# Moving the experts' result stores from the ACT queue to the SP queue

## The reference

```python
E, K, H, CAP = 64, 4, 128, 128          # 64 experts, 4 per token, D = 512
xb = zeros((E, CAP, D)).at[eid, pos].set(flat[tok], mode='drop')
h  = silu(einsum('ecd,edh->ech', xb, Wg)) * einsum('ecd,edh->ech', xb, Wu)
yb = einsum('ech,ehd->ecd', h, Wd)
y  = yb[eid, minimum(pos, CAP - 1)] * (w * valid)[:, None]
out = zeros((N, D)).at[tok].add(y)      # and shared experts are added
```

## Time and profile before

| what | value |
|---|---|
| median of 3 runs | 1286.22 us (1281.49 to 1287.89) |
| the profiled execution | 1287.89 us, span 1286.2 us |
| busy: PE, DVE, ACT, POOL | 85%, 58%, 38%, 44% of the span |
| mean granted TensorE clock | 0.945 |
| `experts` loop | about 947 to 1187 us of the span |
| HBM traffic | 141.23 MB read, 77.59 MB written |

### The profile page before, as it was taken

How to read it: one execution, slowest core, us unless ns; L and a number is a source line. 1 busy time by engine, 2 the same in 40 slices (tenths; PEclk the granted TensorE clock), 3 DMA queues, 4 the chain that set the end, 5 groups by cost and what they waited for, 6 DMA issues and landing times. The chain is left out here.

```text
span 1286.2 us, 19956 instructions
## 1 busy us (share of the span) xinstructions
PE 1095.3 (85%) x5479; PEld 757.0 (59%) x5479; DVE 745.0 (58%) x1760; ACT 486.0 (38%) x865; POOL 570.1 (44%) x754
## 2 busy tenths in 40 slices
PE   3998999999858999997798499999178998888984
PEld 2555555555246777773496276675066766666752
DVE  4678788886337888885556377575412222222565
ACT  2455555555217888885321101212022222221000
POOL 6365565565334666676125456454400000000775
PEclk9999999999958999999799699999679999999988
DMA  9544334541444333332421030220379999995776
GB/s 313 194 164 148 111 125 157 179 163 58 149 150 144 107 107 106 106 106 96 155 67 61 29 110 24 66 75 11 111 262 337 326 355 340 349 349 175 219 234 201
DMA packets 112117, 210.26 MB, mean 163 GB/s; under 512 B 15549, under 2 KB 23741, under 8 KB 112058
## 3 DMA queue, kind: packets, MB, share of 16 engines
q1 hardware_dynamic: 86842, 149.65, 34.8%
q0 software_dynamic: 16000, 43.13, 10.6%
q10 hardware_dynamic: 9216, 16.78, 3.4%
HBM read 141.23 MB, written 77.59 MB: 170 GB/s over the span
## 5 line engine op out<-in xcount | busy, mean ns | idle before, releaser
L1975 POOL DMA_INDIRECT y<-ytab,take x64 | 69.3, 1083 | 275.7 <-POOLq L1814 256.5
L953 POOL TENSOR_TENSOR m_down_lo<-wo,m_down_hi 128x512 fp32r<-128x512 f32 x80 | 133.1, 1683 | 80.6 <-ACT m_down_hi L1028 80.6
L2040 PE MATMUL bank<-flat_hi,w_hi 128*128 128x512 f32 (+1 forms) x320 | 115.8, 362 | 12.9 <-DVE sh_h_b L2051 6.3
L471 PE MATMUL bank<-win,vT 128*128 128x512 f32 x256 | 124.7, 600 | 0.0
L1931 DVE TENSOR_TENSOR stage_gate<-stage_gate,bank 128x128 f32<-128x128 f32 x64 | 18.5, 288 | 166.4 <-ACT stage_gate L1902 166.4
L2040 PE MATMUL bank<-flat_lo,w_hi 128*128 128x512 f32 (+1 forms) x320 | 113.3, 354 | 0.0
L2040 PE MATMUL bank<-flat_hi,w_lo 128*128 128x512 f32 (+1 forms) x320 | 113.0, 353 | 0.0
L641 DVE TENSOR_REDUCE negmax<-bank 128x1 bf16<-128x512 f32 x128 | 86.9, 679 | 41.4 <-PE bank L478 41.0
L564 ACT ACTIVATE win<-bank 128x512 f32<-128x512 f32 x128 | 69.4, 594 | 99.1 <-PE bank L463 98.6
L1042 DVE TENSOR_TENSOR m_up_lo<-w,m_up_hi 128x1024 fp32r<-128x1024 f32 x80 | 99.2, 1241 | 10.3 <-ACT m_up_hi L1015 8.4
L1869 PEld LDWEIGHTS bank<-ident,m_x 128*128 128x128 f32 x256 | 36.7, 208 | 97.2 <-DMA m_x<-tab 86.1
(11 more groups left out here) (286 smaller groups left out, 2601.7 us busy)
## 6 DMA issues: line engine op xcount, KB each, us to landing
m_x<-tab SPq DMA_DIRECT2D x104, 256.0 KB, 3.2
tab<-zeros SPq DMA_DIRECT2D x16, 1024.0 KB, 10.3
ytab<-summary ACTq DMA_DIRECT2D x64, 256.0 KB, 4.9
ytab<-m_y SPq DMA_DIRECT2D x40, 256.0 KB, 2.0
wout<-in_ctx SPq DMA_DIRECT2D x64, 128.0 KB, 2.6
w<-in_L_ffn_wi SPq DMA_DIRECT2D x16, 512.0 KB, 5.4
wo<-in_L_ffn_wo SPq DMA_DIRECT2D x8, 512.0 KB, 6.8
wout<-in_ctx SPq DMA_DIRECT2D x16, 256.0 KB, 3.2
```

What stands on the lines that cost most here:

```text
L471: nc.tensor.matmul(pO[s * 2 + h][:], vT[:, s, sb_, h:h + 2, :].rearrange("p a c -> p (a c)"), probs[:, sb_ % 2, h, :], start=(sb_ == 0), s ...
L953: nc.gpsimd.tensor_tensor(dn_lo[:, m, :], row(wo0, e * MB + m), dn_hi[:, m, :], ALU.subtract).then_inc(dn_lo_ready, 1)
L1975: nc.gpsimd.indirect_dma_start(y1[:, t % RING, k, :], None, T["ytab1"], bass.IndirectOffsetOnAxis(take1[:, t, k:k + 1], 0)).then_inc(gathe ...
L2040: last = nc.tensor.matmul(out, w[:, k, s, wc], x[:, d, cols], start=(d == 0 and part == 0), stop=(d == DB - 1 and part == 2))
```

## The change

The wait for `y_ready` and the issue of the store move from the end of ACT's step to the end of SP's step, behind the loads of the step. The final wait for all stores moves too. The semaphore, the ring and the address stay.

```diff
@@ SP
                 if valid(e, n=E1) and (not isinstance(e, int) or e >= W_EARLY):
                     need(sp, y_full, i)
                     load_expert(sp, A, T, (q - 1) % W_RING, e)
+                if valid(i - 1, n=E1):
+                    n = (q - 1) % RING
+                    need(sp, y_ready, i)
+                    sp.dma_start(T["ytab1"][bass.ds((i - 1) * CAP1, CAP1), :], y[:, n, :]).then_inc(stored[n], 16)
 
             steps(sp, step, E1, W_RING, W_RING - 1, 1)
+            for s in range(RING):
+                sp.wait_ge(stored[s], 16 * E1 // RING)
@@ ACT
                     need(act, h_ready, i - 1)
                     nc.scalar.activation(g[:, s, :], pH[s][:, 0:CAP1], ACT.Silu).then_inc(g_ready, 1)
-                if valid(i - 1, n=E1):
-                    n = (q - 1) % RING
-                    need(act, y_ready, i)
-                    act.dma_start(T["ytab1"][bass.ds((i - 1) * CAP1, CAP1), :], y[:, n, :]).then_inc(stored[n], 16)
 
             steps(act, step, E1, RING, 1, 1)
-            for s in range(RING):
-                act.wait_ge(stored[s], 16 * E1 // RING)
```

## The result

The changed kernel took 1297.72 us in the median of 4 runs (1292.33 to 1299.58), the kernel before 1283.87 in 4 (1281.49 to 1287.89). The ratio is 1.0091, with a 95% interval of 1.0062 to 1.0120: slower by 0.9%, where no change was forecast. It compares means, over 23 executions of the changed kernel; the two medians alone would give 1.0108. The time lies inside the stated range (1273 to 1300), on the side that had a chance of 0.20.

What follows compares the result with a forecast made beforehand. It took DMA and TensorE as coupled, with the rows' landing bounding two loop steps. Terms summed 0 + 0 + 0 + 0 + 0 = 0 against the profiled 1287.89 us; it predicted the median, 1286 us, range 1273 to 1300.

Steps and rivals of the forecast that it cites:

- circle of waits: In the loop, two steps last at least issue delay, rows' landing and one unstalled step: 0.1 + 3.9 + 3.50 = 7.5 us.
- exchange rate: In the loop, a rows' landing longer by x costs x/2 in every step; a shorter one gains x/2 down to 3.50 us.
- unstalled step: A loop step in which TensorE doesn't wait, taken as 3.50 us from the trace, 1098.86 to 1102.36.
- bound of a gain: Most the loop could gain if TensorE's step bound it: (3.77 - 3.50) x 63 = 17 us.
- the traffic: Loop's DMA transfers: same bytes in another order, 0 for the rows' landing, Wd landing sooner; cost 0.
- The store's lateness: Store in the loop issued 1.1 us later, its buffer rewritten only four steps, 15 us, later; cost 0.
- The first rival: Store on q1 ahead of each rows' load counts in full: +20 us, 1306; chance 0.20 together with the clock rival.
- The clock: Second rival: long TensorE stalls lower its clock, 1.5 us each, ten more add 15 us; chance 0.20 with the first rival.
- The faster rival: Rows get the DMA engines for themselves, 0.17 us a step: -10 us, 1276, at most -17; chance 0.24.
- ACT's relief: ACT's queue loses a wait and an issue, 0.34 us per step, covered by TensorE's own work; gain 0.
- SP's issue: Store's issue takes some 0.5 us of SP's queue per step, covered by its 1.72 us slack; cost 0.
- the end of the loop: Last two stores go out on SP behind their copies, before GpSimd starts: 0, give or take 0.3 us.

Runs made afterwards that it cites:

- The square: Store's queue by issue time, against the kernel before (q10, behind Wg): q10 behind Wd 1.0137, q1 behind Wg 1.0062, q1 behind Wd (the changed kernel) 1.0128.
- the pad: Changed kernel with an unused DRAM tensor of 1317 rows between tab1 and ytab1: 1.0112 of the kernel before, the changed kernel beside it 1.0096.

## Why the prediction was wrong

**The bound.** The circle of waits was the right frame, and it was the change's whole loss: with the rows' lead one or two steps longer the changed kernel is 2.1 and 2.5% faster than the one before. Its exchange rate held in size from end to end, not from kernel to kernel. From landing and loads in 180 us: 3.4 and 3.53 us a step (no stores), 3.9 and 3.75 (before), 4.6 and 4.0 (the change), 5.0 and 4.5 (rows alone on ACT). From the first to the last that is 0.6 us of step for each us of landing, where I had 0.5, and a part of the last is the clock; between the kernel before and the change it is 0.36. Rows and stores on ACT don't fit: a landing of 4.6 as in the change, but 41 loads and 4.4 us a step. What was mis-sized in the circle is the unstalled step, 3.50 for 3.21. The step of the earlier trace rows had no wait of TensorE in the rows, but its weight loads had waited 0.93 us for rows. So the bound of a gain was not 17 us but (3.77 - 3.21) x 63 = 35; 0.9755 is 31. With 3.21 the circle gives (0.1 + 3.9 + 3.21) / 2 = 3.6 for the kernel before, where 3.75 was measured: it matched only with the stalled step, so a sum of medians shows the direction better than the size.

**The step that failed: the traffic.** I wrote that engines busy 0.98 of the time "do the same work before the rows either way" and took 0 for the landing. It rose by 0.7 us. The square shows that the moment of the store's issue decides most of this, and that the argument left it out: it counted which transfers have landed when the rows do, and took it for given that the DMA engines get through the same work in the same time. By the same medians the old store was in flight with the next rows for 5.7 - 3.8 = 1.9 us; the late one goes out 2.0 us behind the rows and lands 5.5 later, at 7.5, with the next rows issued at about 4.0, so an estimate is 3.5 us together. They did not: 320 GB/s for 346, at a share of 0.95. Wd did not land sooner either, which was the same error seen from the other side.

**The store's lateness.** I noted 1.1 us of it and asked only for its buffer, four steps away. That was true and beside the point. The measured price of about 1.3 us more is 1.4% on q10 (1.0137).

**The first rival** had the right outcome and landing (4.3 or more; 4.6), but not the waits for loads (above 40 us; 35.9), and a wrong cause in part: it wanted one queue to be the reason, but the late store costs as much on two. Its price was +20 us; 0.91% of 1283.87 is 11.7. By 0.6 x 0.7 the 57 steps should have lost 24 us, while the profiled loops differ by 9.5. In 980 to 1160 the step grew by 0.25 us, over the whole loop by 0.15, since the profiled loop before had lost time in its first steps that the changed one did not.

**The clock.** TensorE's waits reached 2.4 us, and the mean granted clock of the stage was 0.98 (before 0.99): two steps with matmuls of 2.87 and 3.06 us for 1.95, where the kernel before had one of 2.98. So this rival gave about 1 us there. It worked more in the other kernel: the profiled execution before had two slow steps in the first 33 us of the loop, where the changed one had none.

**The faster rival** is refuted twice: with the store on q1 at its old time the rows landed after 4.2 us, not earlier than 3.9, and a queue of their own made them land at 5.0. The rule of the Trainium skill that a DMA engine takes turns between queues ("DMA: Bandwidth & Descriptors", "Queues, rings and completion order") does not contradict that; I may have applied it to the wrong partner. The transfer on the other queue at the time of the rows' issue is then Wg, and taking turns with it would be a loss; no run here shows the turns themselves. The other rule of the Trainium skill, same page, section "Issuing engines are not separate DMA queues", that a second issuer only saves the time of issue, held with early rows (0.9755 against 0.9760) and, in the times, with the late store (1.0128 against 1.0137); at the old time the queue alone made 0.6%.

**What held:** ACT's relief gained nothing, SP's issue was covered, the wait for `y_ready` was free, and the end of the loop cost nothing.

**What stays open** is why the DMA engines get less through of the same five transfers when the store is late. The kernel without stores rules out that a store in the middle merely fills idle time for free; the pad rules out one distance of addresses. What each DMA engine does within the step was not measured. And whether the 0.6% of the queue at the old time is the queue or the slightly later issue (1.0 us behind the rows against 0.7 in the mean) was not separated; the loop of that kernel took 236.1 us in its trace, against 237.7 in the profiled execution before, the slowest of its four, so no trace locates this part.

## What to carry to other kernels

When a load bounds a loop through a circle of waits, count the time from its issue to its use, and first ask whether it can be issued earlier: here the same four buffers allowed two steps more, and that was worth 2.5%, more than any place of the store. Until then, what is issued late in the step and close ahead of that load has a price, even if its own data is in no hurry. "DMA engines 98% busy" did not mean that they were at their limit: the same loop moved 398 GB/s, at a share of 1.05, once it could run ahead.

## What the runs showed of the hardware

A load moved to a queue of its own, issued together with a load on the other queue, landed 0.4 us later than in the changed kernel and 1.1 later than in the one before (5.0, 4.6, 3.9). One queue and two moved the same 398 GB/s of these transfers of 256 KB, at a share of 1.05, when enough was in flight (980 to 1130, rows five experts ahead). With three experts' lead the kernels with all five transfers moved 293 to 346 GB/s at shares of 0.87 to 0.99. With four and five experts' lead the rows landed after 6.4 and 9.4 us: from four to five the lead bought next to no more speed in that stretch (396 and 398 GB/s), only a longer landing.
